# Value products on high and low parts in five of eight halves of a cross-attention and expert kernel

## The reference, cut to what matters

```python
kv_in = concat([layer_norm(ctx), lat], axis=1)      # lat = layer_norm of the normalized tokens
sim = einsum('bhqd,bhfd->bhqf', (lat @ Wq) * scale, kv_in @ Wk)
out = einsum('bhqf,bhfv->bhqv', softmax(masked(sim)), kv_in @ Wv)
x = x + out @ Wo
scores = sigmoid(xn @ gate_w)                       # xn = layernorm(x); the two highest of 8, normalized
h = silu(xn @ w1[e]) * (xn @ w3[e])
x = x + (silu(xn @ ws1) * (xn @ ws3)) @ ws2 + sum_e gate[e] * (h @ w2[e])
```

## Time and profile before

| | before |
|---|---|
| time, median of 3 runs (lowest, highest) | 1110.14 us (1110.12, 1111.85) |
| profiled execution: time, span | 1111.61 us, 1109.8 us |
| mean granted clock of TensorE | 0.992 |
| busy: PE, PEld, DVE, ACT, POOL | 1069.8, 932.5, 924.9, 792.3, 616.0 us |

### The profile page before, as it was taken

One profiled execution on the slowest core, in us unless ns is written; L12 is line 12 of the kernel. 1 busy time (PEld: TensorE's weight loads), 2 busy tenths in 40 slices (PEclk: granted clock), 3 DMA queues, 4 the chain that ended last, 5 costly groups with the idle time before them and its releaser, 6 DMA issues.

```text
span 1109.8 us, 28179 instructions
## 1 busy us (share of the span) xinstructions
PE 1069.8 (96%) x7720; PEld 932.5 (84%) x7720; DVE 924.9 (83%) x4095; ACT 792.3 (71%) x2924; POOL 616.0 (56%) x717
## 2 busy tenths in 40 slices
PE   6799999999999999999999999999999999999985
PEld 5688888888888888888888888888888888888864
DVE  3778888888888888988888898888898888888864
ACT  3777777777777777777777777777777777777730
POOL 4555565656565555655566655555565555664421
PEclk8999999999999999999999999999999999999997
DMA  5355555555555555555555555555555555544531
GB/s 154 124 172 163 162 164 164 171 162 162 172 168 168 164 164 163 172 163 167 163 170 163 158 177 166 165 169 164 157 177 161 168 166 166 164 157 150 167 110 34
DMA packets 248717, 176.81 MB, mean 159 GB/s; under 512 B 29424, under 2 KB 215408, under 8 KB 248560
## 3 DMA queue, kind: packets, MB, share of 16 engines
q1 hardware_dynamic: 244400, 173.71, 52.1%
q10 hardware_dynamic: 4160, 1.31, 0.5%
HBM read 103.35 MB, written 71.56 MB: 158 GB/s over the span
## 4 chain that ended last, share of the span: by engine, by line
PE 91%; DVE 2%; issue 2%; SPq 1%; DMA 1%; ACT 1%; POOL 1%; ACTq 0%; POOLq 0%; DVEq 0%
PE bank L879 19%; PE bank L866 19%; PE bank L821 15%; PE bank L822 14%; PE bank L823 14%; PE bank L827 6%; PE bank L942 1%; PE bank L894 1%; SPq L339 1%; DMA pT<-probsT_dram 1%; PE bank L887 1%; PE bank L931 1%; DMA wk_raw<-in_L_xattn_Wk 1%; PE bank L804 0%; DVE MV_lo L787 0%
## 5 line engine op out<-in xcount | busy, mean ns | idle before, releaser
L451 POOL TENSOR_TENSOR probs<-probs,rdenom 128x512 f32<-128x512 f32 x256 | 266.7, 1042 | 358.0 <-DVE rdenom L685 353.3
L556 ACT ACTIVATE probs<-logits,neg_max 128x128 f32<-128x128 f32 x1024 | 398.9, 397 | 0.9 <-DVE neg_max L676 0.9
L879 PEld LDWEIGHTS bank<-kvT,tT 128*128 128x128 f32 x2048 | 268.0, 191 | 120.0 <-issue 103.9
L879 PE MATMUL bank<-kvT,tT 128*128 128x128 f32 x2048 | 269.8, 275 | 0.0
L866 PE MATMUL bank<-pT,kv_f 128*128 128x512 f32 x512 | 262.5, 594 | 6.6 <-DMA pT<-probsT_dram 6.5
L676 DVE CUSTOM_DVE_ANT_0 logits<-bank,mask_add 128x128 f32<-128x128 f32 x1024 | 232.6, 283 | 6.5 <-PE bank L879 6.3
L721 DVE TENSOR_TENSOR cT_lo<-bank,cT_hi 128x512 fp32r<-128x512 f32 x256 | 175.1, 684 | 58.3 <-ACT cT_hi L525 58.2
L556 ACT ACTIVATION_READ_ACCUMULATOR probs<-logits,neg_max 128x1 f32 x1024 | 197.6, 193 | 0.0
L510 ACT ACTIVATE h_tanh<-bank 128x256 f32<-128x256 f32 x160 | 61.6, 385 | 186.6 <-PE bank L823 184.2
L525 ACT CAST cT_hi<-bank 128x512 fp32r<-128x512 f32 x256 | 150.0, 586 | 45.8 <-PE bank L866 45.7
L691 DVE STREAM_TRANSPOSE probsT<-probs 128x512 f32<-128x512 f32 x256 | 176.0, 687 | 0.7 <-issue 0.5
(11 more groups left out here) (102 smaller groups left out, 1982.3 us busy)
## 6 DMA issues: line engine op xcount, KB each, us to landing
probsT_dram<-probsT SPq DMA_DIRECT2D x256, 256.0 KB, 2.1
pT<-probsT_dram SPq DMA_DIRECT2D x1024, 64.0 KB, 2.1
gates<-gates_dram SPq DMA_DIRECT2D x62, 256.0 KB, 4.3
kv_raw<-in_ctx SPq DMA_DIRECT2D x32, 128.0 KB, 2.8
kv_raw<-in_x SPq DMA_DIRECT2D x32, 128.0 KB, 2.8
mask_raw<-in_mask_BxS_ik SPq DMA_DIRECT2D x32, 128.0 KB, 3.5
x_res<-in_x SPq DMA_DIRECT2D x32, 128.0 KB, 3.4
out<-out_sb SPq DMA_DIRECT2D x32, 128.0 KB, 2.0
```

The source lines that it names most:

```text
L451: nc.gpsimd.tensor_tensor(by_pair, by_pair, rdenom[n][:, :].unsqueeze(2).unsqueeze(3).broadcast_to([P, PAIRS, P // QUAD, QUAD]), ALU.mult) ...
L556: nc.scalar.activation(probs[c % 4][:, :, r, :], logits[c % 2][:, r, :].rearrange("p (c k) -> p c k", k=QUAD), ACT.Exp, bias=neg_max[c % 2 ...
L879: last = nc.tensor.matmul(S_ps[c % 2][:, P * r:P * (r + 1)], tT[:, kl % 4, hd:hd + 2, :], kvT[g % 2][:, kl % 4, :], start=True, stop=True)
```

## The change

In the halves kl = 0, 1, 2, 4 and 6 (`SPLIT_HALVES`; in a frame these are k = 4, 5, 6, 0 and 2) the value product is made by `matmul3` from high and low parts. `kv_f` is split once a group: ACT casts `kv_hi` behind the exponentials of k = 0, POOL subtracts `kv_lo` in k = 1. `pT` is split for each of these halves: ACT casts `pT_hi` ahead of everything else in the half, POOL subtracts `pT_lo` as the first thing in the half. PE makes the product not at the start of the half but behind the logits and query products. The other three halves keep the fp32 product at the start. To make room, `cT_hi` and `cT_lo` are kept once instead of twice; what writes them waits for the projection's first eight heads (`W_front_done`) or its last (`W_in_psum`).

```diff
+        kv_hi = [sb(f"kv_hi{n}", [P, GB, D], f32r) for n in range(3)]
+        kv_lo = [sb(f"kv_lo{n}", [P, GB, D], f32r) for n in range(3)]
+        pT_hi = [sb(f"pT_hi{n}", [P, PAIRS * P], f32r) for n in range(2)]
+        pT_lo = [sb(f"pT_lo{n}", [P, PAIRS * P], f32r) for n in range(2)]
-        cT_hi = [sb(f"cT_hi{n}", [P, GB, 2, PAIRS * P], f32r) for n in range(2)]
-        cT_lo = [sb(f"cT_lo{n}", [P, GB, 2, PAIRS * P], f32r) for n in range(2)]
+        cT_hi = sb("cT_hi", [P, GB, 2, PAIRS * P], f32r)
+        cT_lo = sb("cT_lo", [P, GB, 2, PAIRS * P], f32r)
+        SPLIT_HALVES = (0,1,2,4,6)
...
+        def split_before(c):
+            return len(SPLIT_HALVES) * (c // HALVES) + sum(k < c % HALVES for k in SPLIT_HALVES)
+        def has_split(c):
+            return has_half(c) and c % HALVES in SPLIT_HALVES
... POOL, start of a half
+                    if has_split(e - 4):
+                        c = e - 4
+                        n = split_before(c)
+                        pool.wait_ge(pT_hi_ready, n + 1)
+                        nc.gpsimd.tensor_tensor(pT_lo[n % 2][:, :], pT[c % 3][:, :], pT_hi[n % 2][:, :].bitcast(fp32),
+                                                ALU.subtract).then_inc(pT_lo_ready, 1)
+                    if k == 1 and has(j, p, -1, NG - 2):
+                        g = i + 1
+                        pool.wait_ge(kv_hi_ready, g + 1)
+                        nc.gpsimd.tensor_tensor(kv_lo[g % 3][:, :, :], kv_f[g % 3][:, :, :], kv_hi[g % 3][:, :, :].bitcast(fp32),
+                                                ALU.subtract).then_inc(kv_lo_ready, 1)
... ACT, start of a half
+                    if has_split(e - 4):
+                        c = e - 4
+                        n = split_before(c)
+                        act.wait_ge(pT_loaded[c % 3], 64 * (c // 3 + 1))
+                        after(act, C_in_psum, c - 1)
+                        nc.scalar.copy(pT_hi[n % 2][:, :], pT[c % 3][:, :]).then_inc(pT_hi_ready, 1)
... ACT and DVE, before cT_hi and cT_lo
                         if kl == 0:
-                            after(act, W_in_psum, g - 1)
+                            after(act, W_front_done, g)
+                        if kl == 4:
+                            after(act, W_in_psum, g)
... ACT, behind the exponentials
+                    if k == 0 and has(j, p, -1, NG - 2):
+                        g = i + 1
+                        act.wait_ge(kv_step, KV_STEPS * (g + 1))
+                        after(act, C_in_psum, HALVES * (g - 2))
+                        nc.scalar.copy(kv_hi[g % 3][:, :, :], kv_f[g % 3][:, :, :]).then_inc(kv_hi_ready, 1)
... PE, start of a half
-                    if has_half(e - 4):
+                    if has_half(e - 4) and not has_split(e - 4):
... PE, behind the query product
+                    if has_split(e - 4):
+                        c = e - 4
+                        g, kl = c // HALVES, c % HALVES
+                        n = split_before(c)
+                        pe.wait_ge(pT_lo_ready, n + 1)
+                        if kl == SPLIT_HALVES[0]:
+                            pe.wait_ge(kv_lo_ready, g + 1)
+                        after(pe, cT_lo_ready, c - 1)
+                        matmul3(C_ps[c % 2][:, :], kv_hi[g % 3][:, kl % 4, :], kv_lo[g % 3][:, kl % 4, :],
+                                pT_hi[n % 2][:, :], pT_lo[n % 2][:, :]).then_inc(C_in_psum, 1)
```

More of the change, by code:

```diff
@@ L107, in xattn_moe_ffn_kernel @@
         h_silu = sb("h_silu", [P, GT])
-        h = [sb(f"h{n}", [P, NT + 1, GT]) for n in range(2)]
         out_sb = [sb(f"out_sb{n}", [P, TT, D]) for n in range(2)]
@@ L120, in xattn_moe_ffn_kernel @@
             wT = [su(f"wT{n}", [P, H // 2, D]) for n in range(3)]
-            su("unused", [P, 5 * H * DH])
+            su("unused", [P, H * DH])
             w13_stage = [su(f"w13_stage{n}", [P, (NT + 1) * P]) for n in range(2)]
-        cT_hi = [sb(f"cT_hi{n}", [P, GB, 2, PAIRS * P], f32r) for n in range(2)]
-        cT_lo = [sb(f"cT_lo{n}", [P, GB, 2, PAIRS * P], f32r) for n in range(2)]
+        cT_hi = sb("cT_hi", [P, GB, 2, PAIRS * P], f32r)
+        cT_lo = sb("cT_lo", [P, GB, 2, PAIRS * P], f32r)
+        h = [sb(f"h{n}", [P, NT + 1, GT]) for n in range(2)]
         banks = [es.enter_context(nc.psum_tensor(f"bank{n}", [P, 512], fp32)) for n in range(8)]
@@ L168, in xattn_moe_ffn_kernel @@
         pT_loaded = [sem(f"pT_loaded{n}") for n in range(3)]
+        kv_hi_ready = sem("kv_hi_ready")
+        kv_lo_ready = sem("kv_lo_ready")
+        pT_hi_ready = sem("pT_hi_ready")
+        pT_lo_ready = sem("pT_lo_ready")
         C_in_psum = sem("C_in_psum")
@@ L171, in xattn_moe_ffn_kernel @@
         cT_lo_ready = sem("cT_lo_ready")
+        W_front_done = sem("W_front_done")
         W_in_psum = sem("W_in_psum")
@@ L523, in frame @@
                         if kl == 0:
-                            after(act, W_in_psum, g - 1)
-                        nc.scalar.copy(by_quad(cT_hi[g % 2][:, kl % 4, kl // 4, :]),
+                            after(act, W_front_done, g)
+                        if kl == 4:
+                            after(act, W_in_psum, g)
+                        nc.scalar.copy(by_quad(cT_hi[:, kl % 4, kl // 4, :]),
                                        C_ps[c % 2][:, :].rearrange("p (a r q) -> p a r q", r=PAIRS, q=QUAD)).then_inc(cT_hi_ready, 1)
@@ L719, in frame @@
                         if kl == 0:
-                            after(dve, W_in_psum, g - 1)
-                        nc.vector.tensor_tensor(by_quad(cT_lo[g % 2][:, kl % 4, kl // 4, :]),
+                            after(dve, W_front_done, g)
+                        if kl == 4:
+                            after(dve, W_in_psum, g)
+                        nc.vector.tensor_tensor(by_quad(cT_lo[:, kl % 4, kl // 4, :]),
                                                 C_ps[c % 2][:, :].rearrange("p (a r q) -> p a r q", r=PAIRS, q=QUAD),
-                                                by_quad(cT_hi[g % 2][:, kl % 4, kl // 4, :].bitcast(fp32)),
+                                                by_quad(cT_hi[:, kl % 4, kl // 4, :].bitcast(fp32)),
                                                 ALU.subtract).then_inc(cT_lo_ready, 1)
@@ L918, in frame @@
                             last = matmul3(W_ps.rearrange("p (b q) -> p b q", b=GB), MV_hi[1][:, hd, :], MV_lo[1][:, hd, :],
-                                           head_columns(cT_hi[1 - p][:, :, :, :], hd), head_columns(cT_lo[1 - p][:, :, :, :], hd),
+                                           head_columns(cT_hi[:, :, :, :], hd), head_columns(cT_lo[:, :, :, :], hd),
                                            first=hd == 0, last=hd == H - 1)
+                            if hd == H // 2 - 1:
+                                last.then_inc(W_front_done, 1)
                             if hd == H - 1:
```

## The result

The changed kernel takes 1347.38 us, median of 4 executions (1344.93 to 1348.35), against 1110.13 us of the kernel before (4 executions): 1.2125 times as long, 95% interval 1.2107 to 1.2143, 237 us more. The prediction was 1332 us, range 1265 to 1390. The profiled execution took 1344.93 us, its span is 1343.2 us.

What follows compares the result with a forecast made beforehand. The prediction took PE, busy 96% of the span, as the bound. Four stretches added 7.15 us a frame; 31 frame steps gave 221.7 us on top of 1110.1, so 1332 us, range 1265 to 1390.

Steps and rivals of the forecast that it cites:

- value product of half 7 to half 2: First stretch of PE's frame: product of half 0 waits for pT_lo, query of half 1 for tT; +2.82 us.
- to half 5: Second stretch, from half 2: POOL's late pT_lo delays the product of half 4, DVE's run close behind; +2.02 us.
- to half 6: Third stretch, from half 5: PE and ACT take turns, 5.15 us a half; +0.60 us.
- to half 7: Fourth stretch, from half 6: PE has nothing else for 1.11 us before the attnT transposes; +1.71 us.
- the first two facts of order: PE's query product waits for tT, 1.06 us into a half; ACT's cT_hi stands ahead of attnT, kvT and exponentials.
- The prices: Instruction times taken: split product 0.72 us instead of 0.86, casts 0.48 to the next instruction, pT_lo 1.27.
- Parts costed at nothing: SP's loads of pT, the shared cT buffers and kv_lo on POOL in half 1 were claimed to add no time.
- ACT did not run ahead: Rival: ACT finishes exponentials early, so halves 5 and 6 wait only for tanh and tT; 1305 us, 12%.
- The clock did not fall: Rival: PE's granted clock falls in each frame's first stretch, doubling work behind the waits; 1440 us, 8%.
- POOL did not lengthen DVE's run: Rival: one more instruction of DVE's run waits out a POOL subtraction, half 5 at 15.60; 1364 us, 6%.
- The rival price: Skill's matmul spacing of 131 ns on PE: product 0.39 us, sum 1281 us; no chance of its own given.

Runs made afterwards that it cites:

- Experiment 4: Changed kernel, but the five moved value products are single fp32 matmuls behind the query product, with no high or low parts made: 1257.89 us, ratio 1.1316.
- experiment 2: Changed kernel, but ACT makes attnT ahead of cT_hi instead of behind it in half 6: 1326.58 us, ratio 1.1934.
- experiment 3: Changed kernel, but POOL makes pT_lo of half 0 ahead of x_ve and x_r instead of behind them: 1320.6 us, ratio 1.1881.
- experiment 5: Changed kernel, but kv_hi is cast at the end of half 3 instead of in half 0, and kv_lo made in half 5 instead of 1: 1334.67 us.
- experiment 1: Changed kernel with no half split; kv_hi and kv_lo made but unused, cT buffers still kept once: 1121.62 us, ratio 1.0086 to the kernel before.
- Experiment 7: Changed kernel, but only kl = 1, 2, 3 split, all value products at the head of the half, parts made earlier: 1111.92 us, ratio 1.0011.
- experiment 6: Changed kernel, but POOL's kv_ve and kv_r moved from half 3 to half 4, behind pT_lo: 1362.86 us, ratio 1.2268.
- Experiment 12: Experiment 7's kernel, but split products, casts and subtractions only in frames 3 to 30 of 32: 1102.97 us, ratio 0.9922 to the kernel before.
- experiment 8: Experiment 7's kernel with kl = 7 (half 3) split early too: 1133.58 us, ratio 1.0206.
- run 116: Not a number of a run, 116 is us: kernel before, with only the loads of pT moved ahead of the store of probsT: 1226.8 us, ratio 1.1055.

## Why the prediction was right

**The stretches.** Predicted and measured, us: value product of half 7 to half 2 13.56 and 13.75; to half 5 14.56 and 14.50; to half 6 5.15 and 5.20; to half 7 6.63 and 6.65; the frame 39.9 and 40.10. The waits that it named (for pT_lo in halves 0 and 4, for tT in half 1, for attnT) stand where it put them. The frame was put 0.20 us too short, which is 6.2 us in 31. PE's share of busy time is 84%, not about 80%.

**The term that was left out** is the start. The first transposes of attnT come at 81.2 us before and 93.6 after, the last at 1078.4 and 1313.8 (two matmuls a group; the lines give the later one of the last pair):

```profile
L931 PE MATMUL bank<-ident,attnT x64: 272/272/328, 81.2 to 1078.5; 128*128 128x128 f32 x64
```

```profile
L989 PE MATMUL bank<-ident,attnT x64: 270/274/328, 93.6 to 1313.9; 128*128 128x128 f32 x64
```

So the 31 frame steps grew by 1220.2 - 997.2 = 223.0 us (predicted 221.7), the end fell from 31.4 to 29.4, and the start grew by 12.4: 233.4 together, the difference of the spans. (The medians differ by 237.25, since the profiled execution lay 1.48 us above the median before and 2.45 below it after.) The prediction multiplied the steady frame by 31 and costed what lies ahead of it at nothing.

That the 31 steps came out within 2 us is partly luck. The steps at both ends are shorter than the steady frame, before (30.93 and 31.98 first, 32.48, 29.88 and 20.46 last) as after (37.81 and 39.93; 39.07, 36.63 and 24.12), and the last one grew by only 3.66. Thirty-one times the measured growth of the steady frame, 7.35, would be 227.9: 4.9 too much, which offsets most of the 6.2 too little.

**The place.** Experiment 4 shows the first two facts of order without any part being made, stretch by stretch. Experiments 2, 3 and 5 each take one named wait or one cast out of its stretch, and the stretch shortens by 1.16, 0.84 and 0.49 us, against 1.11, some 0.9 and 0.48. They show that these were on the path, and experiment 2 that a wait removed is not a wait saved: the stretch behind it gave back 0.72.

**The prices.** The three matmuls take 686.40 - 685.70 = 0.70 us (0.72 taken). The first one after a wait has 0.34 to the next instead of 0.23, so the products of halves 0 and 4 take 0.81. pT_lo has 1.27, the casts 0.5 to the next instruction. For attnT the bracket says 0.95; counted from where the next matmul could have started, 691.31 + 0.23 = 691.54, it is 1.12 (1.11 taken).

**Parts costed at nothing.** Loads of pT: no wait in the frame. The shared cT, kv_lo and kv_hi together cost 0.4 us a frame in experiment 1. The prediction had kv_hi in its first stretch, and experiment 5 took 0.49 back by moving it. The 0.4 of experiment 1 is kv_hi's as well, for it lies in half 1 alone. Experiment 7, which keeps the shared cT and kv_lo and has kv_hi elsewhere, is back at 4.65 there (582.38 to 587.03).

**Half 2 to half 5.** The prediction had POOL (14.56) bind here, DVE's run (14.33) just behind. The wait for pT_lo stands at 680.43 as said, and kv_r ends 6.97 us after cT_lo of half 2 (6.98 taken). The reason given for that number was wrong in part: the statistics on which kv_r hangs are done at 586.57 in the frame before, but kv_ve and kv_r start at 590.09 and 590.56, because POOL first has the normalization of the probabilities (from 587.63) and the products with the gates. These wait for DVE's run too, so the number held. DVE is as close as predicted. In the changed kernel h ends at 682.24, and the matmul that needs it starts 0.37 later:

```profile
681.82 0.42 DVE L752 TENSOR_TENSOR h<-h_silu,bank 128x256 f32<-128x256 f32 x1
```

```profile
682.61 0.28 PE L866 MATMUL bank<-x2T_hi,w_hi 128*128 128x256 f32 x1
```

In experiment 6 DVE's run is 0.93 longer and the stretch 0.71 (673.56 to 688.77 = 15.21): 0.22 to spare, where the prediction had 0.23.

**The rivals.** ACT did not run ahead: it waited for every product (L868, 160 times). The clock did not fall, as the window of the frame shows (us, busy us of PE, PEld, DVE, ACT and POOL, granted clock, DMA share):

```profile
655.07:695.17 40.10, 34.45 (x246) 30.06 (x245) 28.66 (x127) 27.02 (x97) 26.50 (x29) 1.00 0.46 136
```

POOL did not lengthen DVE's run in the changed kernel: it took 9.98 us, against 10.00 before (medians: g_tie 0.32, g_keep 0.62, as before). Experiment 6 shows that it was one moved step away, at 15 us. The rival price by the Trainium skill (TensorE: Matmul & The Clock Gate, "Back-to-back issue gap") was a sustained 131 ns for 512 columns; for an isolated matmul of this width the same section gives a gap of about 216 ns. The trace has f32r matmuls of 512 columns every 0.23 us, so it does not meet the first and is nearer to the second.

**What would have worked.** The change did carry a gain of 0.16 us a product. Experiment 12 collects it where parts are ready before the half that needs them and PE is the bound: 8 us of the 13.4 that 28 frames of 0.48 would give. The spans of the profiled executions differ by 8.7 us (1109.8 and 1101.1). Of these 5.8 lie in the 31 frame steps (991.4 us instead of 997.2); the other 2.9 lie ahead of and behind them, where no product is split, so not all of the gain is shown to be theirs.

## What to carry to other kernels

Where one engine is busy 96% and the others wait for it in order, an instruction's place is worth more than its length: moving five products by 1.6 us cost some 146 us, while making each 0.16 us shorter is worth 26 at most. New work on the helping engines belongs a stage ahead of its use, behind what the bound engine needs first, and out of the short frames of the start, as experiments 7 and 12 show; experiments 6 and 8 show that it must also keep clear of DVE where DVE has little room. Before two instructions of a queue are swapped, look for the one that waits for the other to finish, not only to be issued.

## What was not expected of the hardware

- Four DMA issues on ACT's queue of 0.67 to 0.69 us each held the next ACT instruction back by 1.40 us, although the exponentials ran beside them.
- A subtraction of 1.3 us on POOL stretched g_tie from 0.32 to 1.25 us on DVE (experiment 6), and the 16-column g_one from 0.14 to 0.54 (experiment 8, medians); g_tie beside kv_ve, 128x4 wide, was not stretched.
- A PE that waited up to 1.4 us several times in a frame kept a granted clock of 1.00.
- With each load right behind the store that it waits for, the landing time of about 2.2 us came into the loop of nearly every half: 255 waits, 377.9 us in all on SP's queue, where there had been 4, and a run 116 us longer.
